# DRAIN instructions on GpSimd's queue ahead of some indirect scatters

## The reference

```python
mod = (_silu(L0_c) @ L0_wmod).reshape(16, 6, 1, -1)      # sa, ca, ga, sb, cb, gb; |ga|, |gb| at least 0.25
h = _layernorm(x) * (1 + ca) + sa
Q = K = V = h @ Wq + bq
x = x + ga * softmax(Q K^T / sqrt(128)) V
h = _layernorm(x) * (1 + cb) + sb
route = sigmoid(h @ Wr + br)                             # 8 experts, the best one is taken
x = x + gb * max(route) * (gelu(h @ W1[e]) @ W2[e])      # e = argmax(route), W1 128x512, W2 512x128
```

## Time and profile before

| | |
|---|---|
| time, median of 3 runs | 354.69 us (354.61 to 355.04) |
| the profiled execution's own time | 354.34 us |
| its span, first to last instruction | 352.6 us |
| mean granted TensorE clock | 0.986 |
| PE busy | 325.0 us (92%) |
| DVE busy | 278.9 us (79%) |
| ACT busy | 223.5 us (63%) |
| POOL busy | 193.1 us (55%) |
| indirect DMAs of L1406 (rows) | 64, 998 ns each |
| indirect DMAs of L1433 (outputs) | 71, 1055 ns each |

### The profile page before, as it was taken

One profiled execution on the slowest core, in us unless ns is written; L12 is line 12 of the kernel. 1 busy time (PEld: TensorE's weight loads), 2 busy tenths in 40 slices (PEclk: granted clock), 3 DMA queues, 4 the chain that ended last, 5 costly groups with the idle time before them and its releaser, 6 DMA issues.

```text
span 352.6 us, 8419 instructions
## 1 busy us (share of the span) xinstructions
PE 325.0 (92%) x2578; PEld 299.6 (85%) x2578; DVE 278.9 (79%) x1114; ACT 223.5 (63%) x477; POOL 193.1 (55%) x224
## 2 busy tenths in 40 slices
PE   2799999999999999999989898899999999999960
PEld 2388788889888988898878798899999999999960
DVE  5378898898889888988997896899897777877730
ACT  2589987888788878887866585654445454434320
POOL 5016467545754575457525445877566556565661
PEclk9999999999999999999999999999999999999995
DMA  3394124337653666943536612664989554454300
GB/s 113 116 256 104 44 68 131 100 112 121 146 105 104 123 128 188 249 138 111 105 91 224 231 50 87 186 205 134 289 259 307 166 171 120 127 139 125 93 21 4
DMA packets 34493, 49.27 MB, mean 140 GB/s; under 512 B 4320, under 2 KB 26115, under 8 KB 34448
## 3 DMA queue, kind: packets, MB, share of 16 engines
q1 hardware_dynamic: 27504, 31.74, 37.0%
q0 software_dynamic: 6368, 16.92, 12.9%
q10 hardware_dynamic: 576, 0.07, 0.1%
HBM read 28.21 MB, written 20.96 MB: 139 GB/s over the span
## 4 chain that ended last, share of the span: by engine, by line
PE 70%; DVE 13%; ACT 6%; issue 5%; DVEq 2%; DMA 1%; POOL 1%; POOLq 0%; SPq 0%; ACTq 0%
PE mixed L625 14%; PE mixed L525 12%; PE flipped L512 6%; PE side L479 4%; PE scores L502 3%; PE scores L500 3%; PE scores L501 3%; PE side L545 3%; PE side L469 2%; PE scores L609 2%; PE scores L610 2%; PE scores L608 2%; PE side L537 2%; PE side L487 2%; PE flipped L609 2%
## 5 line engine op out<-in xcount | busy, mean ns | idle before, releaser
L1406 POOL DMA_INDIRECT sorted_rows<-payload,slots x64 | 63.9, 998 | 79.8 <-DVE slots L1044 64.9
L1433 POOL DMA_INDIRECT out_dram<-y_out,tokens x71 | 74.9, 1055 | 42.4 <-DVE y_out L1105 25.8
L625 PE MATMUL mixed<-down_slot,hidden 128*128 128x128 f32 x568 | 70.1, 276 | 2.5 <-ACT hidden L804 2.5
L625 PEld LDWEIGHTS mixed<-down_slot,hidden 128*128 128x128 f32 x568 | 66.5, 192 | 3.0 <-ACT hidden L804 3.0
L525 PE MATMUL mixed<-v_sb,probs_t 128*128 128x128 f32 x512 | 69.0, 278 | 0.0
L747 ACT ACTIVATE probs<-scores,row_max 128x512 f32<-128x512 f32 x64 | 44.0, 687 | 35.1 <-DVE row_max L937 33.4
L525 PEld LDWEIGHTS mixed<-v_sb,probs_t 128*128 128x128 f32 x512 | 62.2, 192 | 0.2
L937 DVE TENSOR_REDUCE row_max<-scores 128x1 f32<-128x512 f32 x64 | 44.1, 688 | 19.0 <-PE scores L502 19.0
L789 ACT ACTIVATE f_hi<-side 128x256 fp32r<-128x256 f32 (+1 forms) x39 | 14.3, 366 | 42.8 <-PE side L587 42.8
L512 PE MATMUL flipped<-ident,probs 128*128 128x128 f32 x256 | 39.1, 275 | 0.4 <-ACT probs L747 0.3
L755 ACT ACTIVATE probs_t<-flipped 128x512 f32<-128x512 f32 x64 | 37.9, 594 | 0.0
(11 more groups left out here) (187 smaller groups left out, 768.7 us busy)
## 6 DMA issues: line engine op xcount, KB each, us to landing
rows<-sorted_rows SPq DMA_DIRECT2D x32, 388.0 KB, 3.7
x_tile<-in_L_attn_inputs_dram SPq DMA_DIRECT2D x16, 256.0 KB, 3.2
payload<-stored_gates SPq DMA_DIRECT2D x16, 256.0 KB, 9.3
sorted_rows<-pad_rows SPq DMA_DIRECT2D x9, 388.0 KB, 4.6
w_parts<-in_L_ffn_W_dram SPq DMA_DIRECT2D x1, 2048.0 KB, 8.8
rows<-sorted_rows SPq DMA_DIRECT2D x7, 194.0 KB, 2.6
out_dram<-y_out,tokens POOLq DMA_INDIRECT x71
gate<-stored_gates SPq DMA_DIRECT2D x16, 64.0 KB, 5.8
```

What stands on the lines that cost most here:

```text
L625: last = nc.tensor.matmul(mixed[t % 2][:, u * H:(u + 1) * H], hidden[:, t % 2, f, u * P:(u + 1) * P], down_slot[:, t % 3, f, :], start=(f ...
L1406: nc.gpsimd.indirect_dma_start(rows_dram, bass.IndirectOffsetOnAxis(ap=slots[:, c:c + 1], axis=0), payload[:, b.q, j, :], None).then_inc(s ...
L1433: nc.gpsimd.indirect_dma_start(out_rows, bass.IndirectOffsetOnAxis(ap=tokens[:, t % RING, u:u + 1], axis=0), y_out[:, t % RING, u, :], Non ...
```

## The change

Twelve DRAIN instructions are added to GpSimd's list. Two stand ahead of the row scatters of batches 11 and 13 (B is 16), before the waits for their inputs. Ten stand in `write_out` of tiles 10, 13, 16, 19, 22, 25, 28, 31, 34 and 37, behind the wait for the tile's `y_out` and ahead of its indirect DMAs. Nothing else is changed.

```diff
             def scatter(b):
                 if not real(b):
                     return
+                if b.n in (B - 5, B - 3):
+                    pool.drain()
                 wait(pool, slots_ready, b.n + 1)
...
                 if not real_tile(t):
                     return
                 wait(pool, y_ready, t + 1)
+                if t > 9 and t % 3 == 1:
+                    pool.drain()
                 for u in range(parts(t)):
                     nc.gpsimd.indirect_dma_start(
```

## The result

The changed kernel is slower: 359.62 us (median of 6 runs, 358.06 to 360.73) against 354.87 us (354.59 to 355.69) in the same comparison, a ratio of 1.013 with a 95% interval of 1.011 to 1.015. (The medians in this document are over all runs of a kernel, the ratios over its fast runs alone, those within 1.5% of its fastest, so the two can point different ways where runs spread widely.) The forecast was 349.9 us. In a second comparison it was 358.37 against 354.72 (1.010, 1.008 to 1.012). The profiled execution is the slowest of the six, 360.73 us with a span of 359.0 us; for the kernel before it was 354.34 us with a span of 352.6 us. So the trace has to explain 6.4 us, where the medians differ by 4.8 us.

The account below looks back on a forecast made before the run. TensorE was taken to set the pace mid-kernel, GpSimd's exit DRAIN the last 6 us. A gain of 6.0 us less 1.2 (tail) and 0.1 (rounding) made 4.7 us, span 347.9; the forecast was 349.9 us, range 348.8 to 351.8.

Parts of the forecast that it names:

- The exit DRAIN bounds the end: Kernel's end: everything waits for GpSimd's exit DRAIN, whose 7.18 us behind the last record becomes 1.2, a gain of 6.0.
- Rival (b): Kernel's end: the exit's 6 us belongs to the exit and stays; time 354.9 to 355.9 us, chance 0.08.
- (c): Kernel's end: part of the exit's wait is fixed; with half fixed, about 352.5 to 353.5 us, chance 0.06.
- 53 ns per entry: Every DRAIN: a walk over the indirect DMAs since the last DRAIN, 7.18 us / 135 = 53 ns each, chance 0.80.
- The row DRAINs at nothing: Batches 11 and 13: DRAINs of 2.3 and 0.4 us, hidden in GpSimd's idle 6.21 and 3.90 us.
- The step that failed: Tiles 13 to 31: 0.2 to 0.3 us of walk each, or a few tenths more for a landing, hidden.
- it regains 0.7 to 0.8 us a tile: Expert stage: GpSimd needs 2.6 us per full tile in a TensorE period of about 3.4, so it catches up.
- Rival (a): Expert stage: the DRAIN's price doesn't shrink and GpSimd becomes the bound; time about 410 or 396 us, chance 0.06.
- 2.5 us per DRAIN: Expert stage: the price, 10.2 - 7.7, from which GpSimd would become the bound.
- its own sum of 15.4: Expert stage: GpSimd's us for three full tiles with a 7.2 us DRAIN and 0.79 restart, where TensorE needs 10.2.
- the bounds of 0.1 and 7.2 us: Any inserted DRAIN: its price lies between that of the start DRAIN, 0.1 us, and the exit DRAIN, 7.2 us.
- The tail: Tiles 34 to 38: DRAINs at 34 and 37 wait for landings, delaying the last scatter from 344.22 to 345.4, 1.2 us.

Follow-up runs that it names:

- e2: The changed kernel with every DRAIN removed but one at tile 19: 377.2 us against 374.5 for the kernel before (ratio 1.008).
- e1: The changed kernel without its ten tile DRAINs, only those at batches 11 and 13 left: 373.5 us against 374.5 for the kernel before (0.993).
- e10: The changed kernel with tile DRAINs only at 13, 22 and 31, beside batches 11 and 13: 348.86 us against 354.72 for the kernel before (0.983).

## Why the prediction was wrong

**The exit DRAIN bounds the end, and its price depends on what stands behind it.** Right. It went from 7.18 to 1.3 us, where 1.2 was said, and the earlier trace rows were read rightly. Rival (b), that the 6 us belong to the exit, is out, and so is (c).

**53 ns per entry.** Right for a few entries, by luck: it came from the one point of 135, and that point lies on the flat part. Between 33 and 83 each further entry adds 81 ns. At tile 10 it said 1.7 us; the gap there became 5.06 us, and the scatters went out 4.3 us late and not 1.7. That DRAIN ended 4.3 us behind the scatter's record, with 32 entries, where e2's exit took 2.8 us for 33: with the queues busy (285 GB/s during the hold) the same number costs more. How that splits into a slower landing and a slower walk no run shows.

**The row DRAINs at nothing.** Nearly right: batch 11's ended at 176.79 + 7.53 = 184.32 and its first scatter went out at 185.24, 1.0 us later than before, at no visible price, and e1 shows none either. But this was luck in part. The prediction gave it 2.3 us, and it ended 6.1 us behind GpSimd's last work of its own (178.24). VectorE's wait was long enough to cover nearly all of it.

**The step that failed** is this one: "Tiles 13 to 31: 0.2 to 0.3 us of walk each, or a few tenths more where the previous scatter must land first; hidden in the same way." Each of these DRAINs leaves a gap of 2.1 to 4.0 us. It has three terms, and the prediction had all three in its hands but put them together only for the tail. The last scatter must land. Then comes the walk of four to six entries. These two take 1.3 to 3.2 us behind the scatter's record (the gap less 0.79), and longer where the DMA queues carry more: 1.3 to 1.6 at tiles 19, 31, 34 and 37, with 1 to 44 GB/s during the hold, 1.8 at tile 22 with 148, and 2.0 to 3.2 at tiles 13, 16, 25 and 28, with 190 to 282 GB/s. The holds of tiles 13 and 31 as windows (as the earlier trace rows):

```profile
271.51:274.71 3.20, 3.20 (x31) 3.20 (x29) 2.47 (x7) 1.58 (x3) 0.00 (x1) 1.00 0.89 282
336.30:337.73 1.43, 1.43 (x16) 1.43 (x14) 0.95 (x5) 0.33 (x1) 0.00 (x0) 1.00 0.14 44
```

Then GpSimd starts again, 0.79 us from the DRAIN's end to the scatter. Without a DRAIN the sequencer runs ahead beside the scatter before, and the gap is 0.30. Against that stood "it regains 0.7 to 0.8 us a tile", 2.3 us for three tiles. That was too much as well: GpSimd's idle time between tiles 10 and 37 was 17.9 us, 2.0 us for three tiles, and 15.2 us or 1.7 once the scatters themselves had become slower. So a hold of 2.6 us more than a usual gap, every three tiles, isn't hidden. GpSimd comes late to the next DRAIN, and the holds add up.

**Rival (a) had the mechanism and the wrong price.** It said that GpSimd becomes the bound of the expert stage from 2.5 us per DRAIN on, and gave that 0.06, because it only tried 7.2 us and a walk that grows from 4.5 to 7.0. The 2.5 is the whole hold above a usual gap, restart included (10.2 - 7.7); for the price alone, as in its own sum of 15.4, the point is 10.2 - 8.2 = 2.0 us. Measured are 23.1 / 9 = 2.6 us per DRAIN above a usual gap, just past 2.5, and past the 1.7 for which there was room. That is why the outcome is 359.6 us and not 396 to 410. The price between the bounds of 0.1 and 7.2 us, which the prediction itself named, should have been held against that point.

**The tail** was sized at 1.2 us of delay, for a GpSimd that comes to tile 34 on time. It came there 11 to 13 us behind `y_out`, and the last scatter went out 12.2 us later than before. Whether 1.2 us would have held otherwise isn't shown.

The Trainium skill (PSUM — Partial Sum Buffer, section Engine vs sequencer instructions) says that a drain waits for a fully idle engine. The traces show more: with nothing left to do in GpSimd's own record, the exit DRAIN ends 1.3 to 7.2 us later, and the later the more scatters were issued since the last DRAIN. That this is a walk over them is a reading of that growth; no row shows the walk itself.

## What to carry to other kernels

A DRAIN on GpSimd behind indirect DMAs cost their landing, a time that grew with the number of those not yet drained, and a restart of the sequencer; look at the gap between the scatters, not at the DRAIN's own length. The one at the kernel's exit can be made cheap by a few earlier ones (5.9 us of the whole time, 1.7%, in e10), but each has to be paid out of the engine's slack before the next comes: add up slack and holds over the whole stage, as for any engine that "isn't the bottleneck". When an unknown price has wide bounds, find the price at which the engine becomes the bound and ask on which side of it the known terms already lie.

## What was not expected of the hardware

The price of the DRAIN isn't proportional to the number of DMAs: its end behind the last scatter's record was at 1.66, 2.76, 5.04, 6.83 and 7.18 us for 12, 33, 61, 83 and 135. It is as if there were a limit between 61 and some 90 on what is looked at; no run shows the reason. A second DRAIN right behind the first takes 34 to 41 ns. And three of the chips ran the same kernel 16 to 20 us slower, which hid a difference of 10 us between two of its versions.
